# Attention scores of a graph kernel: the clip moved to GpSimd, the value copy to ScalarE

## What is computed

```python
def _L3_gnn_ref(embeds, rows, cols, qTrans, kTrans, vTrans):
    q = (embeds[rows] @ qTrans).reshape(-1, HEADS, head_dim)
    k = (embeds[cols] @ kTrans).reshape(-1, HEADS, head_dim)
    v = (embeds[cols] @ vTrans).reshape(-1, HEADS, head_dim)
    att = jnp.clip(jnp.einsum('ehd,ehd->eh', q, k), -10.0, 10.0)
    expAtt = jnp.exp(att)
    attNorm = segment_sum(expAtt, rows)[rows]
    res = (expAtt / (attNorm + 1e-08))[:, :, None] * v
    return segment_sum(res, rows)
```

## Time and profile before

| | us |
|---|---|
| median of 3 runs | 2568.54 (2566.19 to 2569.42) |
| the profiled execution, its device time | 2562.42 |
| its span in the trace | 2560.7 |
| share of the span busy: PE, DVE, ACT, POOL | 47%, 73%, 31%, 50% |

### The profile page before, as it was taken

How to read it: one execution, slowest core, us unless ns; L and a number is a source line. 1 busy time by engine, 2 the same in 40 slices (tenths; PEclk the granted TensorE clock), 3 DMA queues, 4 the chain that set the end, 5 groups by cost and what they waited for, 6 DMA issues and landing times. The chain is left out here.

```text
span 2560.7 us, 40050 instructions
## 1 busy us (share of the span) xinstructions
PE 1212.2 (47%) x12261; PEld 593.6 (23%) x12261; DVE 1858.0 (73%) x3971; ACT 785.6 (31%) x1920; POOL 1287.9 (50%) x1016
## 2 busy tenths in 40 slices
PE   1111111111111111111102625899999979889987
PEld 1111111111111111111101202244344422333334
DVE  9999999999999999999841001023212589999996
ACT  0000000021332232231111112000001389999995
POOL 2688788888888888888888781000000210000001
PEclk6555555555555555555556867999999989999997
DMA  7776776667777777765656969989997753333331
GB/s 237 224 217 195 222 219 195 189 150 225 217 195 246 204 212 222 228 163 156 173 154 182 381 206 361 394 333 369 397 345 287 239 146 88 88 87 87 89 86 43
DMA packets 268041, 541.20 MB, mean 211 GB/s; under 512 B 132064, under 2 KB 140701, under 8 KB 258237
## 3 DMA queue, kind: packets, MB, share of 16 engines
q1 hardware_dynamic: 127485, 288.88, 32.3%
q10 hardware_dynamic: 26000, 245.78, 24.5%
q0 software_dynamic: 114480, 5.67, 11.0%
HBM read 371.92 MB, written 168.31 MB: 211 GB/s over the span
## 5 line engine op out<-in xcount | busy, mean ns | idle before, releaser
L1160 POOL DMA_INDIRECT table<-held x782 | 1220.2, 1560 | 331.1 <-issue 307.6
L686 DVE SCALAR_TENSOR_TENSOR resident<-resident,ring,banks 128x1280 bf16<-128x1280 f32 (+9 forms) x790 | 691.9, 941 | 0.3 <-DVE ring L672 0.3
L995 PE MATMUL banks<-ring,resident 128*128 128x6 bf16 x4345 | 128.7, 167 | 1022.3 <-DVE held L695 1022.3
L461 ACT ACTIVATE held<-held 128x128 f32<-128x128 f32 x575 | 171.8, 302 | 762.4 <-DMA weights_dram<-held 752.9
L1109 PE MATMUL banks<-ring,scaled 128*64 128x512 f32 x1250 | 315.6, 620 | 165.2 <-DVE scaled L794 81.1
L995 PEld LDWEIGHTS banks<-ring,resident 128*128 128x128 bf16 x4345 | 122.1, 104 | 1033.7 <-DVE held L695 1033.7
L1436 POOL COPY v_tile<-acc 128x64 f32 x175 | 41.3, 236 | 440.1 <-PE banks_d L1475 439.2
L678 DVE SCALAR_TENSOR_TENSOR scaled<-resident,ring,banks 128x1280 bf16<-128x1280 f32 x156 | 235.2, 1545 | 20.3 <-issue 17.6
L1208 POOL DMA_DIRECT2D parts_dram<-scaled x7 | 5.4, 778 | 449.1 <-DVE scaled L866 448.9
L1460 PE MATMUL banks_d<-held 96*128 (+2 forms) x700 | 192.7, 365 | 42.9 <-ACT att L1337 32.3
L1339 ACT ACTIVATE att<-att,shift 128x1024 f32<-128x1024 f32 (+1 forms) x175 | 208.6, 1192 | 0.0
(11 more groups left out here) (224 smaller groups left out, 1481.9 us busy)
## 6 DMA issues: line engine op xcount, KB each, us to landing
table<-acc ACTq DMA_DIRECT2D x100, 800.0 KB
held<-table ACTq DMA_DIRECT2D x24, 3200.0 KB
ring<-counts_dram SPq DMA_DIRECT2D x60, 1280.0 KB, 13.2
ring<-weights_dram SPq DMA_DIRECT2D x60, 1280.0 KB, 11.9
resident<-keys_dram SPq DMA_DIRECT2D x79, 640.0 KB
weights_dram<-held ACTq DMA_DIRECT2D x25, 1600.0 KB
counts_dram<-c_tile ACTq DMA_DIRECT2D x24, 1600.0 KB, 5.5
count<-counts_dram SPq DMA_DIRECT2D x150, 256.0 KB, 2.7
```

What stands on the lines that cost most here:

```text
L461: ins = nc.scalar.activation(w_tile[:, s], cells[:, s, :, 0], ACT.Copy, accum_out=deg_parts[:, s, bass.ds(t, 1)])
L686: ins = nc.vector.scalar_tensor_tensor(equal[b][:, OWN_AT[j]:OWN_AT[j + 1]], key_row[:, b, j * P:GE], keys[:, bass.ds(g * G + j, 1)], own_ ...
L995: nc.tensor.matmul(sums, equal[b][:, at:at + P], parts_g[:, b, j, :], start=False, stop=True, skip_group_check=True)
L1160: nc.gpsimd.indirect_dma_start(out=table, out_offset=bass.IndirectOffsetOnAxis(ap=cell[:, slot, j:j + 1], axis=0), in_=amount[:, slot, j, ...
```

## The change

It touches the score loop. ScalarE takes Exp of both pairs of heads straight out of PSUM, without bias, and then copies the values into `v_tile`, which GpSimd did. GpSimd clips each pair in place in SBUF with one two-operation instruction (min with e^10, then max with e^-10). VectorE only multiplies each pair by the counts. The order of the pairs is high, low on every engine. PE's program is as it was.

```diff
@@ ScalarE
+            act.wait_ge(v_cleared, 3)
                 def exps(t, j, n, u):
                     act.wait_ge(values_added, u + 1)
-                    act.wait_ge(scored[1], u + 1)
-                    nc.scalar.activation(att[:, j, high, 0:W], scores[:, high, 0:W], ACT.Relu, bias=shift[:, 0:1]
-                                         ).then_inc(scores_read[1], 1)
-                    act.wait_ge(scored[0], u + 1)
-                    nc.scalar.activation(att[:, j, low, 0:W], scores[:, low, 0:W], ACT.Exp).then_inc(scores_read[0], 1)
-                    act.wait_ge(scores_read[1], u + 2)
-                    nc.scalar.activation(att[:, j, high, 0:W], att[:, j, high, 0:W], ACT.Exp, bias=shift[:, 1:2]
-                                         ).then_inc(expd_high, 1)
+                    for f in (1, 0):
+                        act.wait_ge(scored[f], u + 1)
+                        nc.scalar.activation(att[:, j, pairs[f], 0:W], scores[:, pairs[f], 0:W], ACT.Exp
+                                             ).then_inc(scores_read[f], 1)
+                    nc.scalar.copy(by_head[:, j, :, 0:HD],
+                                   values[:, bass.ds(t, 1)].rearrange("p a (h f) -> p (a h) f", h=HEADS)
+                                   ).then_inc(value_taken, 1)
@@ VectorE
                 def weigh(t, j, n, u):
-                    dve.wait_ge(scores_read[0], u + 2)
-                    nc.vector.tensor_scalar(att[:, j, low, 0:W], att[:, j, low, 0:W], HI, LO, ALU.min, ALU.max
-                                            ).then_inc(clipped, 1)
                     dve.wait_ge(counts_turned, u + RING + 1)
-                    dve.wait_ge(expd_high, u + 1)
                     times = count_t[j % 3][:, 0:W].unsqueeze(1).to_broadcast([P, 2, W])
-                    nc.vector.scalar_tensor_tensor(att[:, j, high, 0:W], att[:, j, high, 0:W], HI, times,
-                                                   ALU.min, ALU.mult)
-                    dve.wait_ge(clipped, u + 1)
-                    nc.vector.tensor_tensor(att[:, j, low, 0:W], att[:, j, low, 0:W], times, ALU.mult
-                                            ).then_inc(weighted, 1)
+                    for f in (1, 0):
+                        dve.wait_ge(clipped[f], u + 1)
+                        ins = nc.vector.tensor_tensor(att[:, j, pairs[f], 0:W], att[:, j, pairs[f], 0:W], times, ALU.mult)
+                    ins.then_inc(weighted, 1)
@@ GpSimd
-                def take(t, j, n, u):
-                    pool.wait_ge(values_added, u + 1)
-                    nc.gpsimd.tensor_copy(by_head[:, j, :, 0:HD],
-                                          values[:, bass.ds(t, 1)].rearrange("p a (h f) -> p (a h) f", h=HEADS)
-                                          ).then_inc(value_taken, 1)
+                def clip(t, j, n, u):
+                    for f in (1, 0):
+                        pool.wait_ge(scores_read[f], u + 2)
+                        pool.sem_inc(clipping, 1)
+                        nc.gpsimd.tensor_scalar(att[:, j, pairs[f], 0:W], att[:, j, pairs[f], 0:W], HI, LO,
+                                                ALU.min, ALU.max).then_inc(clipped[f], 1)
```

More of the change, by code:

```diff
@@ L57 @@
 EPS = 1e-5
-CLIP = 10.0
 RING = 5
@@ L1242, in attention_layer @@
     att = sb("att", [P, RING, HEADS, BANK], F32, c)
-    shift = sb("shift", [P, 2], F32, c)
+    shift = sb("shift", [P, 1], F32, c)
     o_t = sb("o_t", [P, NR], F32, c)
@@ L1249, in attention_layer @@
     scores, acc, count_t = banks[:, 0:4], banks[:, 4], [banks[:, n] for n in (5, 6, 7)]
+    by_head = v_tile[:].rearrange("p j (h f) -> p j h f", h=HEADS)
     LO, HI = 4.5399929762484854e-05, 22026.465794806718
@@ L1258, in attention_layer @@
     scores_read = [sem(f"scores_read{f}") for f in range(2)]
-    expd_high, clipped = sem("expd_high"), sem("clipped")
+    clipped = [sem(f"clipped{f}") for f in range(2)]
+    clipping = sem("clipping")
     value_taken = sem("value_taken")
@@ L1284, in over_chunks @@
         chunk(SC, T - 4 * SC)
-    low, high = slice(0, 2), slice(2, 4)
+    pairs = (slice(0, 2), slice(2, 4))
     LOOPED = (T - 2) // RING * RING
@@ L1323, in _ @@
             act.wait_ge(consts_set, 2)
-            nc.scalar.activation(stat[:, 0, 0:1], shift[:, 1:2], ACT.Exp)
+            nc.scalar.activation(shift[:], shift[:], ACT.Exp)
+            act.wait_ge(v_cleared, 3)
             for f in range(2):
@@ L1355, in _ @@
             nc.vector.memset(zero_row[:], 0.0).then_inc(consts_set, 1)
-            nc.vector.memset(shift[:, 0:1], CLIP)
-            nc.vector.memset(shift[:, 1:2], -CLIP).then_inc(consts_set, 1)
+            nc.vector.memset(shift[:], 0.0).then_inc(consts_set, 1)
             dve.sem_inc(weighted, 2)
@@ L1423, in _ @@
         def _(pool):
-            by_head = v_tile[:].rearrange("p j (h f) -> p j h f", h=HEADS)
             nc.gpsimd.memset(v_tile[:], 0.0).then_inc(v_cleared, 1)
@@ L1432, in chunk @@
             def chunk(ci, width):
-                def take(t, j, n, u):
-                    pool.wait_ge(values_added, u + 1)
-                    nc.gpsimd.tensor_copy(by_head[:, j, :, 0:HD],
-                                          values[:, bass.ds(t, 1)].rearrange("p a (h f) -> p (a h) f", h=HEADS)
-                                          ).then_inc(value_taken, 1)
-                over_tiles(pool, ci, take)
+                W = columns(width)
+                def clip(t, j, n, u):
[4 more added lines that the diff above has]
+                                                ALU.min, ALU.max).then_inc(clipped[f], 1)
+                over_tiles(pool, ci, clip)
             over_chunks(pool, chunk)
```

## The result

| | before | changed |
|---|---|---|
| median, us | 2567.8 (4 runs, 2566.2 to 2569.4) | 2481.6 (4 runs, 2481.0 to 2486.6) |
| ratio | 1 | 0.967, 95% interval 0.965 to 0.969 |
| profiled execution: device time, span | 2562.4, 2560.7 | 2481.0, 2479.3 |

The changed kernel is 3.3% faster, 86 us by the medians and 81 us by the two profiled executions. Other sets of runs of the kernel before, taken with the experiments, had medians of 2565.3 and 2564.6, so the gain is known to some 3 us. The sign and the mechanism held; one term of the sum was too large.

What follows compares the result with a forecast made beforehand. PE was to bound the wide steps at 2.57 us instead of 2.95: 150 x (2.95 - 2.57) = 57 us saved, less 2 at edges, so 2568.5 - 55 = 2513 us. The range was 2495 to 2635 us.

Steps and rivals of the forecast that it cites:

- No gap: Wide steps before the change: VectorE's three starts, 1.13, 0.69 and 1.13 us apart, were read as filling the 2.95 us period.
- The clip: GpSimd in the wide steps: each clip of 1024 elements was taken at 1.03 us, so 2.06 us a step.
- The upper bound of 1.94: Slowest GpSimd clip, 1.94 us at 1.78 ns an element: step 3.88 us, 2710 us; slow-clip rival's chance 0.25.
- VectorE and ScalarE: Wide steps: VectorE's two products need 2.26 us; ScalarE's two Exps and value copy need 2.04 us.
- rival 3: GpSimd's clips and VectorE's products exclude each other in SBUF: wide step 4.3 us, +200 us, 2770 us; chance 0.03.
- The rings: Wide-step dependency loops through Exps: three steps with clips and product, 2.34 us a step; two steps through PE, 2.42.
- PE's floor: PE's own work in a wide step without waits: 2.44 us, or 2.65 with score pairs apart; 2.57 was taken.
- five terms: Wide-step needs compared: VectorE 2.26, ScalarE 2.04, GpSimd 2.06, the rings 2.34 and 2.42, PE 2.44 to 2.65 us.
- Edges: Wide-step starts and ends: 1.0 us for a first-tile clip, about 0.2 at each of six chunk ends; 2 us lost.
- The narrow steps: 25 steps of the score loop: two clips take 0.57 us, hidden under PE's 1.12 us period; costed at nothing.

## Why the prediction missed, by its own steps

**The reading of before.** Right that ScalarE was full and PE had 0.30 to spare. "No gap" on VectorE was wrong by 0.09 us: it needed 2.86 of the 2.95 and was close behind, not a second bound. It made no difference to the sum, since that pass goes away; it made the expectation for the experiment without the third pass miss.

**The clip.** 1.03 us taken, 1.04 measured as duration and 1.00 from start to start. For 128 elements it took 293 ns, so 0.83 ns an element and a fixed 0.19. Reading copy and select as one rate with one fixed cost came near (the rows gave 0.73 ns; 0.83 was my choice above them, no row's). The upper bound of 1.94 was far off, and with it a quarter of the chances. The 1.03 cycles of the Trainium skill (GPSIMD Engine Reference, 3.1, Elementwise) are an estimate of 0.86 ns at its 1.2 GHz; the trace's 0.83 agrees within 3%. Its 1.8 cycles, 1.5 ns, did not show in this instruction.

**VectorE and ScalarE.** 2.26 taken, and two products in 2.26 seen where they bound the loop. ScalarE's Exps start 0.92 apart (0.90 taken), and its copy takes 0.246 (0.24 taken).

**GpSimd against VectorE (rival 3).** The products take 1217 ns in the changed kernel, and 1218 where three clips a step fill GpSimd, as they did beside a nearly idle one. No contention showed.

**The rings.** 2.34 and 2.42 taken. The second was too high, as the step of 2.40 lies below it; with less on PE the loop went to 2.27 and stopped at VectorE. They were never the bound.

**PE's floor: the step that failed.** The rows gave 2.44, and I set against it an upper value of 2.65, for the case that the pairs of scores stay apart, and took 2.57 between them because "five terms are this close". The step is 2.40. What had kept the pairs apart was ScalarE: with three passes it gave the second pair's banks back 0.30 us too late. The kernel without the third pass shows four scores in one block of 1.04, and so does the changed kernel; the kernel before with the bf16 turn still has them apart. That wait was part of what the change removes, and the 2.65, which leaves out the wait of 0.30, still keeps what the split costs PE (the full 0.60 of the first pair). So the upper value rested on a split whose cause I had already counted as gone, and for 2.57 between the two no row spoke. 0.17 us x 150 = 25 us: that is the miss in the wide steps.

**Edges.** 2 us taken. 150 x 0.551 would be 82.7, and 77.5 came, so 5 us were lost at starts and ends. At the six chunk ends the restart is a chain: a chunk now takes 61.86 us, 25 x 2.404 and 1.76; before it took 75.27, 25 x 2.955 and 1.40. That accounts for 2.2 of the 5. Most of the rest is the clock, which the prediction had at 1.00 throughout. The first two chunks took 63.66 and 63.49 us, together 3.4 more than twice 61.86, and of that the kernel before has only 0.2. In each of them the granted clock was at its lower level for a stretch, and a block of four scores took 1.89 us there in place of 1.04:

```profile
2065.00:2070.00 5.00, 5.00 (x20) 1.80 (x18) 3.44 (x4) 3.12 (x5) 3.65 (x4) 0.51 0.55 128
2132.00:2134.50 2.50, 2.50 (x12) 0.66 (x5) 1.79 (x2) 1.02 (x3) 1.68 (x2) 0.50 0.36 105
```

```profile
2132.84 1.89 PE L1457 MATMUL banks_d<-held 96*128 x4
```

Why it fell at the start of the second chunk, after a wait of 1.13 us for the clearing of `acc`, and not at the later ones with the same wait, was not shown; the kernel with the copy on GpSimd took 61.62 and 61.87 for its first two chunks, and 375.8 for all wide steps. These losses offset the miss a little, by chance. The narrow steps, taken at nothing, gave 1.5.

With 2.40 for 2.57 and 5 for 2, the sum is 78 us, 2490. Of the 8 or 9 us that are left, 1.5 lie in the narrow steps and 2.3 in the tables of the two profiled executions. The other 5 are the distance of the medians of before from its profiled execution (2567.8 against 2562.4), which the changed kernel doesn't have (2481.6 against 2481.0): I had taken that distance as alike in both. The larger sets of runs put the median of before at 2565.3 and 2564.6, so some half of these 5 us is scatter of a small set. The tables' 2.3 look like scatter too: the same tables are ready for the first scores between 2059.7 and 2064.7 us in the ten traces, and the changed kernel has the earliest.

## What to carry to other kernels

Where two engines are full at nearly the same time, relief of one shows next to nothing: the clip alone moved gave 0.0%, the third pass alone left out 0.5%, both 3.3%. Which of the two is the bound can hide in overlapping durations, as VectorE's wait of 0.09 us did here: a duration of 0.69 against 0.60 from start to start where nothing waits. After such a change take the floor of the next engine from the stretch of the old trace where it runs with no wait, and don't add to it the waits that the change removes, nor what they cost the engine in split work. Then ask which work of that engine can be had for less time: here bf16 products for fp32 transposes, worth nothing before the change and 0.75% after it.

## What the runs showed of the hardware

- GpSimd's two-operation clip in fp32 runs at 0.83 ns an element on 128 partitions (1040 ns for 1024, 293 for 128), 1.00 us from start to start, beside DVE products that read one operand from PSUM, without slowing them (1217 ns, 1218 beside a full GpSimd).
- VectorE's clip of 1024 fp32 elements in SBUF holds it 0.60 us; a duration of 0.69 contains the start of the next.
- Four 128x128 transposes in fp32 hold PE 0.53 us, four products with a bf16 identity 0.32.
- PE ran four score products in 1.04 us at a granted clock of 1.00 and in 1.89 us at 0.50.
- Executions of the kernel before differ in PE's mean granted clock without a difference in time: spans of 2564.4 and 2562.9 us at 0.965, of 2561.7 and 2563.9 us at 0.697. Where the difference lies can be seen between the profiles of two kernels: the clock digits in the making of the tables, where PE mostly waits, are 9 in that of the kernel with the clip alone moved (mean clock 0.963) and 5 in that of the kernel before.
